# Attention and quantised feed-forward on one core: value matmuls of two key steps in one visit, with a fourth score bank and a ring of three

## The chip, the core and the metric

The kernel runs on one core of a Trainium2 chip. The metric is the device time of one execution in microseconds: 2210.75 us before, the median of three runs from 2209.54 to 2210.94. The engines are TensorE (PE, its weight loads shown as PEld), VectorE (DVE), ScalarE (ACT), GpSimd (POOL) and SyncE (SP), which issues all DMAs.

## The reference

One layer on x of shape (4, 2048, 256), float32. Attention with 16 heads of width 16, causal over the 2048 positions; then a matrix product whose operands are rounded in blocks of 32 to a 6-bit grid.

```python
x = x + attention(layernorm(x), Wq, Wk, Wv, Wo, bo)
x = x + ffn(layernorm(x), weight, bias)

def attention(x, Wq, Wk, Wv, Wo, bo):          # B, C, E = 4, 2048, 256; H, D = 16, 16
    q, k, v = (heads of x @ Wq, x @ Wk, x @ Wv)
    scores = where(causal, q @ k.T, -inf)
    return (softmax(scores / sqrt(E)) @ v) @ Wo + bo

def ffn(x, weight, bias):
    # blocks of 32: scale = max|block| / 7.5, values to the nearest point of the fp6 e2m3 grid
    return dequantised(x) @ dequantised(weight).T + bias
```

## The kernel before, in words

Four heads form a key group; there are 16 groups (4 batches by 4), and each has four query chunks of 512 (a *chunk* k below). For a chunk the kernel walks over the blocks of 128 keys that it can see: 4, 8, 12 or 16 of them, 40 *steps* in a group and 640 in all (`STEPS`, lines 53 to 61). In the first eight or so steps of a chunk, blocks on the diagonal stand between full ones; a diagonal block uses only 512, 384, 256 or 128 columns.

The program runs in *slots*, one for each step and some before and after (line 84). In slot p, each engine does in an order that is written out by hand:

- TensorE (lines 1335 to 1344): for each of the four heads h the score matmul of step p (bf16, transposed scores of 128 keys by up to 512 queries, line 1209), and a share of the slot's units. After h = 1 comes the *value visit*: the values of step p - 2 (line 1226), four fp32 matmuls with 17 output rows each, which lie beside each other in the array, one for each head. Each is issued as two instructions. At the end of the slot come the slot's *items*: projections, transposes, output and feed-forward matmuls.
- A *unit* (line 1191) is a score matmul in the other orientation, 128 queries by up to 512 keys; on the diagonal a mask is added by line 1196. It runs about 21 steps ahead of the step that uses it. VectorE reduces it to one maximum for each query (line 947). The maxima of a chunk are combined, split in three bf16 parts by GpSimd, transposed and loaded as extra rows under the queries, so that the score matmul subtracts them.
- ScalarE (lines 867 to 877) takes exp of each score tile into one of four `probs` buffers (line 805), copies items that it empties, and after a chunk's last step copies the accumulator (line 812).
- GpSimd zeroes the triangle of a diagonal step's probabilities (line 645), one slot after its exponentials, and works on normalisation and on the splitting of projections.
- VectorE (lines 1153 to 1166) takes the slot's units in four shares, with the last slot's items behind the first share, projection work behind the second, and output work behind the third.

PSUM has eight banks. Three hold score tiles in turn: score n waits for exponential n - 3 (line 1208). One holds the accumulator. Four form a *ring* that units and items use in the order of their issue: use n waits until use n - 4 has been emptied by its reader (`emptied`, line 489). A value visit waits for the step's exponentials or, on the diagonal, its mask; the first of a chunk also waits for the copy of the accumulator (line 1224). In ScalarE the first exponential of step s waits for the values of step s - 4 (line 803).

Of the kernel before, what the change touches and what calls it, by code (L numbers as in the profile page):

```python
# [8 lines left out]
ACT = mybir.ActivationFunctionType  # L9
# [7 lines left out]
CHUNK = 512  # L17
# [40 lines left out]
NS = len(STEPS)  # L58
# [3 lines left out]
NPROBS = 4  # L62
# [183 lines left out]
for k in range(NK):  # L246
    p = vector(MAX_DONE[k], 0.3, "maximum", k)
    p = pool(p + 1, 0.9, "split_max", k)
    p = item(p + 1, 0.15, "turn_max", k)
# [3 lines left out]
    p = item(done_at + 1, 0.45, "turn_acc", k)  # L253
# [7 lines left out]
for b in range(B):  # L261
    if b + 1 < B:
        for c in range(QC):
            n = QC * (b + 1) + c
            PROJECTED[n] = place_project(n, 160 * b + 4 + 30 * c)
            assert PROJECTED[n] + 3 < 160 * b + 138 + 6 * c, (n, PROJECTED[n])
    for c in range(QC):
        n = QC * b + c
# [8 lines left out]
for g in range(NG):  # L277
    for c in range(QC):
        p = max(GROUP_STEPS * (g - 1) + 2 + 3 * c, -PRO)
        n = QC * (g // QC) + c  # L280
        p = max(p, PROJECTED[n] + 1)
# [5 lines left out]
SLOTS = range(-PRO, max(p for kind, p in AT) + 3)  # L287


SCORE_BANKS, ACC_BANK, RING_BANKS = [0, 1, 2], 3, [4, 5, 6, 7]  # L290
RING = len(RING_BANKS)

ITEM_KINDS = ("turn_max", "turn_acc", "turn_x", "project", "project_v", "turn_weights", "turn_ctx", "attend", "turn_xd",
              "feed")
# [40 lines left out]
def layer_kernel(nc, x, wq, wk, wv, wo, bo, wf, bf, out):  # L335
# [7 lines left out]
    with ExitStack() as stack:  # L343
# [27 lines left out]
        probs = [sbuf(f"probs{u}", [HG, CHUNK]) for u in range(NPROBS)]  # L371
# [31 lines left out]
        for w in range(2):  # L403
            taken[0] = 0
            s = 1 - w
# [53 lines left out]
        probs_ready = sem("probs_ready")  # L459
# [24 lines left out]
        def wait(eng, semaphore, value):  # L484

            if value > 0:
                eng.wait_ge(semaphore, value)
# [306 lines left out]
        @block.scalar  # L794
        def _(act):
            act.wait_ge(zeros_ready, 1)

            def probabilities(s, h):
                k, kb = STEPS[s]
                a = max(kb - TILES * QCS[k], 0) * P  # L800
                n = s * HG + h
                if h == 0:
                    wait(act, values_done, s - NPROBS + 1)
                act.wait_ge(scores_ready, n + 1)
                nc.scalar.activation(probs[s % NPROBS][:, h, a:CHUNK], bank[SCORE_BANKS[n % 3]][:, a:CHUNK], ACT.Exp,  # L805
                                     scale=SCALE).then_inc(probs_ready, 1)

            def copy_acc(k):
                act.wait_ge(values_done, FIRSTS[k] + SIZES[k])
                if k:  # L810
                    act.wait_ge(for_vector, ITEM_NO["turn_acc", k - 1])
                nc.scalar.copy(acc_sb[:, :], acc_bank).then_inc(acc_copied, 1)  # L812

            def take_turned_max(k):
                act.wait_ge(for_scalar, ITEM_NO["turn_max", k])
                wait(act, row_loaded[k % 2], 48 * (k // 2))
                nc.scalar.copy(max_rows[k % 2][0:LEVELS * HG * TILES, :],
                               ring_bank(ITEM_USE["turn_max", k])[0:LEVELS * HG * TILES, :].bitcast(BF16)[:, 0:P]
                               ).then_inc(scalar_emptied, 1)

            def take_turned_x(n, e):
                act.wait_ge(for_scalar, ITEM_NO["turn_x", n, e])
                nc.scalar.copy(xnT[n % 2][:, e, :], ring_bank(ITEM_USE["turn_x", n, e])).then_inc(scalar_emptied, 1)  # L823

            def take_projected(n, m):
                r = 4 * n + m
                act.wait_ge(for_scalar, ITEM_NO["project", n, m])
                wait(act, low_ready, r - 1)
                nc.scalar.copy(proj[r % 2], ring_bank(ITEM_USE["project", n, m])).then_inc(scalar_emptied, 1)  # L829

            def take_projected_v(n, j):
                act.wait_ge(for_scalar, ITEM_NO["project_v", n, j])
                wait(act, v_stored[n % 2], 16 * (n // 2))
                nc.scalar.copy(v_out[n % 2][:, :, 2 * j:2 * j + 2, :, 0:D],
                               ring_bank(ITEM_USE["project_v", n, j])
                               .rearrange("p (j g h d) -> p g j h d", j=2, g=H // HG, h=HG)
                               ).then_inc(scalar_emptied, 1)

            def take_turned_ctx(n, e):
                w = out_set(n)  # L840
                before, times = before_in_set(n)
                act.wait_ge(for_scalar, ITEM_NO["turn_ctx", n, e])
                if before is not None:
                    act.wait_ge(for_vector, ITEM_NO["feed", before, 1])
                nc.scalar.copy(outT[w][:, e, :], ring_bank(ITEM_USE["turn_ctx", n, e])).then_inc(scalar_emptied, 1)

            def take_turned_xd(n, e):
                act.wait_ge(for_scalar, ITEM_NO["turn_xd", n, e])
                act.wait_ge(for_vector, ITEM_NO["attend", n, 1])
                nc.scalar.copy(outT[out_set(n)][:, e, :], ring_bank(ITEM_USE["turn_xd", n, e])  # L850
                               ).then_inc(scalar_emptied, 1)

            def take_items(p):
                for k, in at("turn_max", p):
                    take_turned_max(k)
                for n, e in at("turn_x", p):
                    take_turned_x(n, e)
                for n, m in at("project", p):
                    take_projected(n, m)
                for n, j in at("project_v", p):  # L860
                    take_projected_v(n, j)
                for n, e in at("turn_ctx", p):
                    take_turned_ctx(n, e)
                for n, e in at("turn_xd", p):
                    take_turned_xd(n, e)

            for p in SLOTS:
                if p == 0:
                    act.wait_ge(wf_ready, 1)
                for h in range(HG):  # L870
                    if 0 <= p < NS:
                        probabilities(p, h)
                    if h == 0:
                        take_items(p - 1)
                for k in range(NK):
                    if p == FIRSTS[k] + SIZES[k] + 1:
                        copy_acc(k)

        @block.vector
        def _(dve):  # L880
# [100 lines left out]
            def take_items(p):  # L981
                for k, in at("turn_acc", p):
                    normalise(k)
                for nothing in at("turn_weights", p):
                    take_turned_weights()
                for n, a in at("attend", p):
                    dve.wait_ge(x_again[out_set(n)], 16 * (before_in_set(n)[1] + 1))
                    add_to_x(n, a, "attend")
                for n, a in at("feed", p):
                    add_to_x(n, a, "feed")  # L990
# [161 lines left out]

            for p in SLOTS:
                units = UNITS_AT.get(p, [])
                for i in range(4):
                    for n in share(units, i, 4):
                        take_unit(n)
                    if i == 0:
                        take_items(p - 1)

                    if i == (1 if p >= 0 else 3):
                        projection_work(p)
                    if i == 2:
                        output_work(p)
                for k, in at("maximum", p):
                    maximum(k)
                for step, in at("weights", p):
                    if step == 0:
                        split_bias()
                        scale_weights()  # L1170
                    else:
                        round_weights()

        @block.tensor
        def _(pe):
# [24 lines left out]
            def scores(s, h):  # L1200
                k, kb = STEPS[s]
                g, qc = divmod(k, QC)
                u, a, n = g % 2, max(kb - TILES * qc, 0) * P, s * HG + h
                if s == FIRSTS[k] and h == 0:
                    pe.wait_ge(row_loaded[k % 2], 48 * (k // 2 + 1))
                    if k == 0:
                        pe.wait_ge(rows_of_ones, 2)
                wait(pe, probs_ready, n - 2)
                nc.tensor.matmul(bank[SCORE_BANKS[n % 3]][:, a:CHUNK],  # L1209
                                 k_rows[u][0:ROWS + LEVELS, h, kb * P:(kb + 1) * P],  # L1210
                                 q_rows[u][0:ROWS + LEVELS, qc, h, a:CHUNK],
                                 start=True, stop=True).then_inc(scores_ready, 1)
# [122 lines left out]
            for p in SLOTS:  # L1335
                units = UNITS_AT.get(p, [])
                for h in range(HG):
                    if 0 <= p < NS:
                        scores(p, h)
                    for n in share(units, h, HG):  # L1340
                        unit(n)
                    if h == 1 and 0 <= p - 2 < NS:
                        values(p - 2)
                items(p)

# [21 lines left out]
```

## Time and profile before

| | before |
|---|---|
| median of three runs | 2210.75 us |
| the profiled execution | 2213.29 us, span 2211.6 us |
| PE busy | 2067.0 us, 93% |
| DVE busy | 1671.3 us, 76% |
| ACT busy | 1342.8 us, 61% |
| POOL busy | 790.3 us, 36% |
| mean granted TensorE clock | 0.978 |

Busy times of the engines overlap. The span is the time from the first to the last instruction of the profiled execution; the execution's own time is a little longer. Matmuls are pipelined: an instruction's time reaches over the start of the next one, so the pace of PE is read from the distance between starts.

### The profile page before, as it was taken

The page shows a single profiled execution, that of the slowest core. Times are in us where ns is not written, and L with a number is a line of the kernel's source. Part 1 is how long each engine was busy: PE and PEld are TensorE (multiplying, and loading weights), DVE is VectorE, ACT ScalarE, POOL GpSimd, SP SyncE. Part 2 cuts the span into 40 slices and gives each one's busy share as a digit, 9 for nine tenths or more (in the row PEclk, how much of TensorE's full clock was granted, in tenths as well). Part 3 has the DMA queues.
Part 4 walks back from the last instruction along what each step waited for, and adds up shares of the span by engine and source line. Part 5 has one row for each costly group of instructions (what it writes and reads, how often), then busy time and mean ns, then how long its engine had stood idle before and what let it go on. Part 6 is the DMA issues. An engine that isn't in the chain of part 4 may idle for free.

```text
span 2211.6 us, 36629 instructions
## 1 busy us (share of the span) xinstructions
PE 2067.0 (93%) x13061; PEld 861.3 (39%) x13061; DVE 1671.3 (76%) x3026; ACT 1342.8 (61%) x2881; POOL 790.3 (36%) x1077
## 2 busy tenths in 40 slices
PE   2789999999999999999999999999999999999973
PEld 1334343343334343443434344343434333343432
DVE  5587777868886868787697877777888888888754
ACT  1136666667665657666675766656676666666640
POOL 4313233241333525334433443535232232323232
PEclk8899999999999999999999999999999999999986
DMA  2341130404031141402213141131303030210111
GB/s 92 120 126 51 48 97 28 109 28 107 6 90 32 57 106 38 125 31 59 85 42 83 45 109 47 47 107 39 108 4 104 4 101 7 71 37 6 51 41 41
DMA packets 180753, 139.79 MB, mean 63 GB/s; under 512 B 56406, under 2 KB 180572, under 8 KB 180572
## 3 DMA queue, kind: packets, MB, share of 16 engines
q1 hardware_dynamic: 180572, 137.45, 22.7%
q8 instruction: 104, 1.70, 0.3%
q14 instruction: 77, 0.63, 0.1%
HBM read 85.73 MB, written 50.86 MB: 62 GB/s over the span
## 4 chain that ended last, share of the span: by engine, by line
PE 81%; DVE 9%; issue 2%; ACT 2%; SPq 2%; POOL 2%; DMA 1%; POOLq 0%; ACTq 0%; DVEq 0%
PE psum L1226 22%; PE psum L1209 22%; PE psum L1191 18%; PE psum L1268 7%; PE psum L1261 5%; DVE max_parts L947 4%; PE psum L1196 2%; PE psum L1251 2%; PE psum L1244 1%; SPq L543 1%; DVE out_shop L1114 1%; DMA shop<-in_L_attn_x 1%; ACT probs L805 1%; PE psum L1290 1%; ACT acc_sb L812 1%
## 5 line engine op out<-in xcount | busy, mean ns | idle before, releaser
L947 DVE TENSOR_REDUCE max_parts<-psum 128x1 f32<-128x512 f32 (+3 forms) x2240 | 1380.1, 667 | 403.4 <-PE psum L1196 210.2
L805 ACT ACTIVATE probs<-psum 128x512 f32<-128x512 f32 (+3 forms) x2560 | 1231.1, 538 | 694.9 <-PE psum L1209 687.4
L1191 PE MATMUL psum<-k_rows,q_rows 96*128 96x512 bf16 (+3 forms) x2560 | 839.3, 349 | 23.8 <-DVE max_parts L947 16.6
L1209 PE MATMUL psum<-q_rows,k_rows 99*128 99x512 bf16 (+3 forms) x2560 | 854.3, 351 | 2.6 <-ACT probs L805 1.9
L1226 PE MATMUL psum<-probs,v_in 128*17 128x512 f32 (+3 forms) x5120 | 594.3, 536 | 10.4 <-ACT acc_sb L812 8.3
L1209 PEld LDWEIGHTS psum<-q_rows,k_rows 99*128 99x128 bf16 x2560 | 237.1, 97 | 621.2 <-ACT probs L805 463.6
L645 POOL TENSOR_SCALAR_AFFINE_SELECT probs<-probs 128x512 f32<-128x512 f32 x256 | 165.0, 645 | 854.2 <-ACT probs L805 854.1
L1191 PEld LDWEIGHTS psum<-k_rows,q_rows 96*128 96x128 bf16 x2560 | 250.6, 98 | 223.5 <-DVE max_parts L947 80.7
L1196 PE MATMUL psum<-maskb,identb 128*128 128x128 bf16 x1024 | 198.7, 220 | 0.0
L1226 PEld LDWEIGHTS psum<-probs,v_in 128*17 128x17 f32 x5120 | 86.1, 95 | 216.7 <-issue 145.8
L1196 PEld LDWEIGHTS psum<-maskb,identb 128*128 128x128 bf16 x1024 | 101.1, 99 | 68.8 <-issue 0.7
L684 POOL CAST neg_max<-neg_rest 128x16 bf16<-128x16 f32 x64 | 12.7, 198 | 223.1 <-DVE neg_rest L954 223.1
L1251 PE MATMUL psum<-ident,shop 128*128 128x128 f32 x160 | 24.8, 305 | 59.4 <-DVE shop L1007 30.3
L676 POOL TENSOR_TENSOR shop<-shop 128x512 bf16<-128x512 f32 x64 | 74.7, 1167 | 5.2
L1261 PE MATMUL psum<-shop,w_q 128*128 128x512 f32 x128 | 64.7, 635 | 2.1 <-ACT shop L823 1.7
L1261 PE MATMUL psum<-shop,w_k 128*128 128x512 f32 x128 | 63.7, 621 | 0.3 <-DVE max_parts L947 0.3
L732 POOL TENSOR_TENSOR out_shop<-out_shop 128x512 f32<-128x512 f32 x28 | 36.8, 1314 | 72.2 <-DVE out_shop L1093 72.1
L829 ACT COPY shop<-psum 128x512 f32<-128x512 f32 x64 | 37.2, 581 | 41.0 <-PE psum L1261 39.4
L675 POOL CAST shop<-shop 128x512 bf16<-128x512 f32 x64 | 40.0, 625 | 61.9 <-DVE shop L1016 60.4
L1268 PE MATMUL psum<-w_v,shop 128*128 128x256 f32 x256 | 61.9, 385 | 0.0
L977 DVE TENSOR_TENSOR out_shop<-psum,out_shop 128x512 f32<-128x512 f32 x56 | 38.2, 683 | 30.9 <-PE psum L1268 30.9
L660 POOL TENSOR_SCALAR shop<-shop,moments,inv_dev 128x256 f32<-128x256 f32 x48 | 58.9, 1236 | 0.6
(116 smaller groups left out, 1353.8 us busy)
## 6 DMA issues: line engine op xcount, KB each, us to landing
qk_scratch<-shop SPq DMA_DIRECT2D x64, 384.0 KB, 2.9
q_rows<-qk_scratch SPq DMA_DIRECT2D x384, 64.0 KB, 2.4
k_rows<-qk_scratch SPq DMA_DIRECT2D x384, 64.0 KB, 2.4
shop<-in_L_attn_x SPq DMA_DIRECT2D x18, 512.0 KB, 4.4
v_scratch<-shop SPq DMA_DIRECT2D x16, 544.0 KB, 3.8
v_in<-v_scratch SPq DMA_DIRECT2D x64, 136.0 KB, 2.4
ctx_scratch<-ctx_out SPq DMA_DIRECT2D x64, 128.0 KB, 1.7
out_shop<-ctx_scratch SPq DMA_DIRECT2D x56, 128.0 KB, 3.1
```

The costliest lines, as they stand in the source:

```text
L645: nc.gpsimd.affine_select(out=tri, in_=tri, compare_op=ALU.is_ge, fill=0.0, base=0, pattern=[[0, HG], [1, P]], channel_multiplier=-1).then ...
L660: ins = nc.gpsimd.tensor_scalar(x_in[n % 2][:, j, :], x_in[n % 2][:, j, :], moments[:, j, 0:1], inv_dev[:, j:j + 1], ALU.subtract, ALU.mult)
L676: nc.gpsimd.tensor_tensor(out=parts[v][:, 2, :], in0=proj[v], in1=parts[v][:, 1, :], op=ALU.subtract).then_inc(low_ready, 1)
L805: nc.scalar.activation(probs[s % NPROBS][:, h, a:CHUNK], bank[SCORE_BANKS[n % 3]][:, a:CHUNK], ACT.Exp, scale=SCALE).then_inc(probs_ready, 1)
L947: nc.vector.tensor_reduce(max_parts[k % 2][:, first:first + heads, t % TILES, c], ring_bank(UNIT_USE[n])[:, 0:heads * width] .rearrange("p ...
L1191: ins = nc.tensor.matmul(dst[:, i * width:(i + 1) * width], q_rows[u][0:ROWS, qc, first + i, t % TILES * P:(t % TILES + 1) * P], k_rows[u] ...
L1196: ins = nc.tensor.matmul(dst[:, (i + 1) * width - P:(i + 1) * width], identb[:, :], maskb[:, :], start=False, stop=True)
L1209: nc.tensor.matmul(bank[SCORE_BANKS[n % 3]][:, a:CHUNK], k_rows[u][0:ROWS + LEVELS, h, kb * P:(kb + 1) * P], q_rows[u][0:ROWS + LEVELS, qc ...
L1226: ins = nc.tensor.matmul(psum[32 * h:32 * h + VW, ACC_BANK, a:CHUNK], v_in[u][:, kb, h * VW:(h + 1) * VW], probs[s % NPROBS][:, h, a:CHUNK ...
L1251: ins = nc.tensor.transpose(ring_bank(use)[:, j * P:(j + 1) * P], t[:, j, e * P:(e + 1) * P], ident[:, :])
L1261: ins = nc.tensor.matmul(ring_bank(use), w[:, e, (m % 2) * P:(m % 2 + 1) * P], xnT[n % 2][:, e, :], start=e == 0, stop=e == EH - 1)
L1268: ins = nc.tensor.matmul(ring_bank(use)[:, j * E:(j + 1) * E], xT[:, e, t * P:(t + 1) * P], w[:, e, :], start=start and e == 0, stop=e == ...
```

## The change

PSUM is dealt out anew: four score banks in place of three, and a ring of three in place of four. The values of an even step and of the odd step after it are issued together, in the visit of the odd slot (step p - 3 and then p - 2); even slots have no visit. ScalarE and VectorE take the last slot's items at the beginning of a slot, before the first exponential and before the first share of units.

```diff
--- before.py
+++ after.py
@@ -287,8 +287,8 @@
 SLOTS = range(-PRO, max(p for kind, p in AT) + 3)
 
 
-SCORE_BANKS, ACC_BANK, RING_BANKS = [0, 1, 2], 3, [4, 5, 6, 7]
-RING = len(RING_BANKS)
+SCORE_BANKS, ACC_BANK, RING_BANKS = [0, 1, 2, 3], 4, [5, 6, 7]
+NSCORE, RING = len(SCORE_BANKS), len(RING_BANKS)
 
 ITEM_KINDS = ("turn_max", "turn_acc", "turn_x", "project", "project_v", "turn_weights", "turn_ctx", "attend", "turn_xd",
               "feed")
@@ -802,7 +802,7 @@
                 if h == 0:
                     wait(act, values_done, s - NPROBS + 1)
                 act.wait_ge(scores_ready, n + 1)
-                nc.scalar.activation(probs[s % NPROBS][:, h, a:CHUNK], bank[SCORE_BANKS[n % 3]][:, a:CHUNK], ACT.Exp,
+                nc.scalar.activation(probs[s % NPROBS][:, h, a:CHUNK], bank[SCORE_BANKS[n % NSCORE]][:, a:CHUNK], ACT.Exp,
                                      scale=SCALE).then_inc(probs_ready, 1)
 
             def copy_acc(k):
@@ -868,10 +868,10 @@
                 if p == 0:
                     act.wait_ge(wf_ready, 1)
                 for h in range(HG):
+                    if h == 0:
+                        take_items(p - 1)
                     if 0 <= p < NS:
                         probabilities(p, h)
-                    if h == 0:
-                        take_items(p - 1)
                 for k in range(NK):
                     if p == FIRSTS[k] + SIZES[k] + 1:
                         copy_acc(k)
@@ -1152,11 +1152,10 @@
 
             for p in SLOTS:
                 units = UNITS_AT.get(p, [])
+                take_items(p - 1)
                 for i in range(4):
                     for n in share(units, i, 4):
                         take_unit(n)
-                    if i == 0:
-                        take_items(p - 1)
 
                     if i == (1 if p >= 0 else 3):
                         projection_work(p)
@@ -1205,8 +1204,8 @@
                     pe.wait_ge(row_loaded[k % 2], 48 * (k // 2 + 1))
                     if k == 0:
                         pe.wait_ge(rows_of_ones, 2)
-                wait(pe, probs_ready, n - 2)
-                nc.tensor.matmul(bank[SCORE_BANKS[n % 3]][:, a:CHUNK],
+                wait(pe, probs_ready, n - NSCORE + 1)
+                nc.tensor.matmul(bank[SCORE_BANKS[n % NSCORE]][:, a:CHUNK],
                                  k_rows[u][0:ROWS + LEVELS, h, kb * P:(kb + 1) * P],
                                  q_rows[u][0:ROWS + LEVELS, qc, h, a:CHUNK],
                                  start=True, stop=True).then_inc(scores_ready, 1)
@@ -1339,7 +1338,8 @@
                         scores(p, h)
                     for n in share(units, h, HG):
                         unit(n)
-                    if h == 1 and 0 <= p - 2 < NS:
+                    if h == 1 and p % 2 and 0 <= p - 3 < NS:
+                        values(p - 3)
                         values(p - 2)
                 items(p)
```

## Rows read from the trace of the kernel before

**Rows 1.** The page: busy time and share by engine, and the granted clock in slices.
```profile
PE 2067.0 (93%) x13061; PEld 861.3 (39%) x13061; DVE 1671.3 (76%) x3026; ACT 1342.8 (61%) x2881; POOL 790.3 (36%) x1077
...
PEclk8899999999999999999999999999999999999986
```

**Rows 2.** Groups by line and shape: busy us, mean ns | idle before.
```profile
L947 DVE TENSOR_REDUCE max_parts<-psum 128x1 f32<-128x512 f32 x1792 | 1130.2, 681 | 223.1 <-PE psum L1191 187.9 <-PE psum L1196 31.7
```

**Rows 3.** Waits: who waited for whom, us in total, times, longest.
```profile
PEld psum L1191 <- DVE max_parts L947: 80.7, 170, 3.2
...
PEld psum L1226 <- POOL probs L645: 10.0, 25, 1.6
...
PE psum L1226 <- ACT acc_sb L812: 8.3, 27, 0.7
```

**Rows 4.** Timeline of one full step: start us, us, engine, line, operation, count.
```profile
1002.82 1.05 PE L1226 MATMUL psum<-probs,v_in 128*17 128x512 f32 x8
...
1003.26 0.61 PE L1226 MATMUL psum<-probs,v_in 128*17 128x512 f32 x4
...
1003.80 0.39 PE L1209 MATMUL psum<-q_rows,k_rows 99*128 99x512 bf16 x1
...
1004.03 0.38 PE L1191 MATMUL psum<-k_rows,q_rows 96*128 96x512 bf16 x1
...
1004.23 2.07 ACT L805 ACTIVATE probs<-psum 128x512 f32<-128x512 f32 x4 [0.80 <-PE psum L1209]
...
1004.25 0.38 PE L1209 MATMUL psum<-q_rows,k_rows 99*128 99x512 bf16 x1
...
1004.45 2.48 DVE L947 TENSOR_REDUCE max_parts<-psum 128x1 f32<-128x512 f32 x4 [0.51 <-PE psum L1191]
...
1005.34 0.38 PE L1191 MATMUL psum<-k_rows,q_rows 96*128 96x512 bf16 x1
...
1005.65 0.13 PEld L1226 LDWEIGHTS psum<-probs,v_in 128*17 128x17 f32 x8 [0.43 <-ACT probs L805]
...
1005.65 1.05 PE L1226 MATMUL psum<-probs,v_in 128*17 128x512 f32 x8
```

**Rows 5.** Timeline of a value visit of 256 columns.
```profile
1117.27 0.63 PE L1226 MATMUL psum<-probs,v_in 128*17 128x256 f32 x8
...
1117.83 0.23 PE L1209 MATMUL psum<-q_rows,k_rows 99*128 99x128 bf16 x1
```

**Rows 6.** Stretches of two steps: start:end, length, busy time by engine, clock, DMA, GB/s.
```profile
135.52:141.50 5.98, 5.78 (x42) 2.08 (x41) 5.98 (x11) 2.82 (x8) 1.27 (x2) 1.00 0.39 108
...
1095.32:1101.23 5.91, 5.91 (x40) 2.07 (x38) 4.42 (x12) 4.34 (x10) 3.15 (x4) 1.00 0.02 2
1101.23:1106.75 5.52, 5.50 (x39) 1.87 (x39) 4.24 (x9) 4.38 (x10) 4.32 (x8) 1.00 0.01 3
1106.75:1112.33 5.58, 5.58 (x40) 2.35 (x40) 4.64 (x9) 3.82 (x10) 0.64 (x1) 1.00 0.09 27
1112.33:1117.27 4.94, 4.94 (x37) 1.94 (x36) 4.91 (x11) 3.44 (x9) 2.56 (x3) 1.00 0.00 0
1117.27:1122.43 5.16, 5.16 (x38) 1.88 (x37) 5.16 (x9) 3.50 (x9) 0.77 (x2) 1.00 0.02 3
1122.43:1127.29 4.86, 4.86 (x33) 1.50 (x32) 4.79 (x10) 3.80 (x9) 0.83 (x4) 1.00 0.00 0
1127.29:1132.98 5.69, 5.69 (x39) 1.94 (x39) 5.18 (x9) 4.67 (x10) 3.31 (x3) 1.00 0.02 2
1132.98:1138.45 5.47, 5.47 (x38) 1.87 (x37) 3.95 (x8) 4.03 (x9) 4.21 (x4) 1.00 0.01 1
1138.45:1144.12 5.67, 5.67 (x35) 1.82 (x34) 4.81 (x9) 4.23 (x9) 0.00 (x0) 1.00 0.01 3
1144.12:1149.71 5.59, 5.32 (x36) 1.81 (x35) 4.50 (x10) 3.98 (x10) 2.35 (x3) 1.00 0.57 137
...
2132.77:2139.21 6.44, 6.44 (x40) 3.13 (x39) 0.36 (x1) 5.16 (x10) 0.00 (x0) 1.00 0.24 83
```

## The prediction

> **What bounds the kernel now.** I read the page first, then the groups of instructions, the waits, one undisturbed step in order of time, and the table of stretches. TensorE is busy for 93% of the span and its granted clock is full through nearly all slices, while VectorE has 76% [rows 1]. The average hides what matters. In steps without projections the table of stretches has PE full, but VectorE is at 4.91 of 4.94 us and 5.16 of 5.16 us in some pairs of steps and at 3.95 of 5.47 us in others [rows 6]. So TensorE sets the pace and VectorE, which reduces the score tiles to maxima ("units") out of the PSUM ring, is level with it for about a third of the pairs. TensorE does wait for VectorE's ring banks, 80.7 us in 170 waits of its weight loads, part of it under running matmuls [rows 3].
>
> **What merging removes.** In the undisturbed step PE starts an instruction of 512 columns every 0.22 us (1004.03 to 1004.25). From the last unit matmul to the first value matmul it is 0.31 us (1005.34 to 1005.65): 0.09 too many. A value visit is two groups of four parallel matmuls 0.44 us apart (1002.82, 1003.26), then the next score matmul at 1003.80: 0.54 after the second group, 0.10 too many [rows 4]. So a visit costs 0.19 us over its streaming, and 640 visits become 320: 320 x 0.19 = 61 us less on PE where PE sets the pace. The second step's groups should follow at 0.44 us.
>
> Whether they do hangs on their weight loads. All eight loads of a visit are done in 0.13 us at its start, and the second group starts 0.44 us after the first, with no gap for a load [rows 4]; a third group isn't shown. Its loads cost nothing (as the second group's) or 0.10 us a pair (the exit bubble again), 0 to 32 us; I take 0, since the second group is the nearest row. The Trainium skill, "TensorE: Matmul & The Clock Gate", section "Step-by-step: what each phase is for", says that a load is pulled ahead of running matmuls if it goes to the background weight buffer or to other row groups; one background buffer would hold the second group, so by this rule the third group's loads could be pulled under the second group's streaming, which gives the same 61 us.
>
> The wait of the first value step of a chunk for ScalarE's copy of the accumulator (8.3 us in 27 waits) [rows 3] goes: PE now gets there a slot later. That is at most 8 us more. The even step's mask on GpSimd also has a slot more, the odd step's none; of those 10.0 us [rows 3] I count nothing, as the odd step ends the visit's wait.
>
> **What it adds: a longer visit over a shorter ring.** VectorE gets nothing new while PE is in a visit. In the chain, PE's last unit before the visit may start once the reduction three uses earlier (four before) has ended; VectorE then has three units in hand. With full widths PE needs 0.31 us from that unit to the visit, 0.98 for the first step's values, 0.88 for the second's, 0.23 for a score, and VectorE starts 0.42 us after the next unit starts (1004.03 to 1004.45): 2.82 us. A reduction takes 0.60 us in a row, (2.48 - 0.68) / 3 [rows 2, 4]; three last 1.80. VectorE therefore starves 1.02 us in each pair. Before, it was 1.94 us of PE against four units or 2.40, so none. With a second step of 256 columns, which costs PE 0.56 us in place of 0.98 [rows 5] and so some 0.44 less, the hole is 0.58. Other VectorE work can lie in the hole (projection statistics of odd slots, normalising, additions to x), which shortens it; units of 384 columns lengthen it. The hole lies between 0 (enough other work there) and 1.02. I take 0.85, nearer to the end with full widths, because in two thirds of the steps the values are full and most of VectorE's other work stands at other places of its slot.
>
> Where PE has that time to spare it costs nothing. Where VectorE is level, the pair lasts VectorE's work plus the hole. So each pair becomes the larger of (its time - 0.19) and (its VectorE time + 0.85). In the ten pairs in a row from 1095.32 [rows 6]: 5.91, 5.52, 5.47 and 5.59 us lose 0.19 each; 5.58 becomes 5.49; 4.94 becomes 5.76; 5.16 becomes 6.01; 4.86 becomes 5.64; 5.69 becomes 6.03; 5.67 becomes 5.66. That is -0.86 and +2.79, or +1.9 us in 54.4. The other half of this key group, with more projection and output matmuls, comes to -0.35. Done for all 319 stretches from 135.52 to 2139.21 (the first and last are in [rows 6]), 113 pairs gain 72 us and the rest lose 35: +37 us, the 61 us already taken off. With a hole of 1.02 it is +65, with 0.4 it is -16, with 0 it is -50.
>
> **The fourth score bank and ScalarE.** Four exponentials take 2.07 us [rows 4], eight 4.14 of a pair of 5.64. While PE is in the long visit ScalarE can have four scores in hand, 2.07 us. From the last score before the visit it is 0.22 us to the last unit, and then the same 2.82 less a few hundredths to the first exponential after it, some 2.8 to 3.0 in all, so ScalarE starves 0.7 to 0.95 and needs 4.9 to 5.1 us a pair: under PE's 5.45. With three banks it would have been 5.4 to 5.6, so the fourth is what keeps the long visit from being ScalarE's bound. It costs the ring its fourth. Cost 0; where two copies of 0.6 us fall in a pair, PE has their matmuls too.
>
> **The moved items.** ScalarE and VectorE now empty the last slot's ring items before the slot's first exponential and unit. PE issues them in that order already, so no engine waits for something later; an exponential is delayed by a copy at most, inside ScalarE's slack (4.0 us busy in pairs of 5.4 [rows 6]). No DMA is issued at another place; SP's waits on scores and values fall at the same slots, as each key group has an even number of steps. ScalarE's wait for the probability buffer four steps back stands behind the next score, which PE issues after that visit anyway. 0.
>
> **Sum.** On the profiled execution, 2213.3 us (span 2211.6): +37 for visits and ring together, -8 at most for the accumulator, of which I take all, gives 2242. The median of the runs is 2.5 below the profiled execution, so 2240.
>
> **Rivals.**
> (a) The hole is filled or hidden, and the bubbles decide: 2160 to 2175, say 2165 (hole 0: 2210.75 - 50, and some of the 8). For it: VectorE has 24% of the span free [rows 1] and some 1 us a pair of work that isn't units (4.64 us busy against seven or eight units). Against it: pairs with VectorE full are those with no spare time for any hole [rows 6], and the order of its work is fixed, so what stands behind a unit can't move ahead into the hole.
> (b) Both effects cancel: a hole of 0.5 to 0.6 gives -5 to +5, and the accumulator's wait makes it 2200 to 2215. For it: many visits have a narrow step [rows 5].
> (c) The three-bank ring costs more than the hole: an item copied by ScalarE takes one of three banks, so VectorE has two units in hand, the hole grows by 0.60, and PE waits also away from visits. If that holds in a third of the pairs, 107 x 0.60 x a half that VectorE decides = 32 us on top: 2270. It decides as soon as a hole exceeds about 1.0. For it: PE already waits 170 times with four banks [rows 3].
> (d) The third group's loads are not hidden: up to 32 us on any of these where PE decides, some 15 on the sum.
> The Trainium skill, "TensorEngine Tiling (Array Packing)", section "PSUM Bottleneck", warns that packing narrow matmuls side by side speeds up TensorE but not the emptying of PSUM, which may then be the bound; this trace agrees in the pairs where VectorE is at 4.91 of 4.94 us [rows 6], and it is the rule that speaks against the change.
>
> **Chances.** The forecast (2220 to 2260) 0.43; (a) 0.26; (b) 0.13; (c) with (d) 0.18. This kernel's measurement tells 0.2%, 4.4 us, from no change. Faster: all of (a) and 0.04 of (b), 0.30; the same 0.08; slower 0.62. The likeliest case has its own range 2220 to 2260; the range for 8 in 10 reaches from (a)'s low end, 2160, to 2285, the sum with a hole of 1.02 and loads that aren't hidden in part.
>
> **What would show it.** Right: value groups come 16 instructions at a time with groups 0.44 us apart and some 1.86 us from first value to next score; pairs such as the one of 5.47 us shrink by 0.19; VectorE has an idle stretch of 0.6 to 1.0 us in each visit, and pairs that were 4.94 and 5.16 us last 5.6 to 6.0; waits of unit matmuls on reductions at least double from 80.7 us; the accumulator's wait is gone. Wrong: if those pairs stay near 5.0 us, VectorE isn't starved and (a) holds; if the third group starts 0.54 us after the second, (d); if waits of score matmuls on exponentials appear in undisturbed steps, ScalarE is the bound and my pricing of the banks was wrong.

## The result, and the profile after

The changed kernel takes 2346.52 us (median of four runs, 2344.76 to 2349.58) against 2210.85 us: ratio 1.0614, 95% interval 1.0595 to 1.0632. That is 136 us slower, outside the range given. The direction was right and the size wrong by more than a factor of four.

The page of the kernel after: busy time by engine, and the granted clock in slices. It answers to [rows 1].

```profile
PE 2132.3 (91%) x13061; PEld 874.6 (37%) x13061; DVE 1666.2 (71%) x3026; ACT 1328.5 (57%) x2881; POOL 789.1 (34%) x1077
...
PEclk8889999999999999999999999999999999999996
```

VectorE does the same work (1666 us) in a longer span. The clock slices look almost the same, but the mean granted clock fell from 0.978 to 0.966.

The waits of the kernel after for VectorE's maxima (us in total, times, longest); the first answers to 80.7 us in 170 waits in [rows 3].

```profile
PEld psum L1190 <- DVE max_parts L947: 381.7, 893, 2.7
...
PE psum L1190 <- DVE max_parts L947: 50.5, 120, 2.2
...
PEld psum L1225 <- POOL probs L645: 8.0, 36, 0.4
```

The masks' row is 8.0 us where it was 10.0. The row of the accumulator's copy, 8.3 us before, has no counterpart any more.

One merged visit and the pair of steps after it, in order of time (start us, us, engine), to be set beside [rows 4]:

```profile
1195.40 1.90 PE L1225 MATMUL psum<-probs,v_in 128*17 128x512 f32 x15
...
1196.27 0.12 PEld L1225 LDWEIGHTS psum<-probs,v_in 128*17 128x17 f32 x4 [0.31 <-issue]
...
1197.24 0.61 PE L1208 MATMUL psum<-q_rows,k_rows 99*128 99x512 bf16 x2
...
1197.67 4.03 ACT L805 ACTIVATE probs<-psum 128x512 f32<-128x512 f32 x8 [1.50 <-PE psum L1208]
...
1198.22 3.68 DVE L947 TENSOR_REDUCE max_parts<-psum 128x2 f32<-128x512 f32 x6 [1.58 <-PE psum L1195]
...
1199.56 0.10 PEld L1190 LDWEIGHTS psum<-k_rows,q_rows 96*128 96x128 bf16 x1 [0.35 <-DVE max_parts L947]
...
1200.16 0.10 PEld L1190 LDWEIGHTS psum<-k_rows,q_rows 96*128 96x128 bf16 x1 [0.49 <-DVE max_parts L947]
...
1200.76 0.10 PEld L1190 LDWEIGHTS psum<-k_rows,q_rows 96*128 96x128 bf16 x1 [0.48 <-DVE max_parts L947]
...
1201.08 0.62 PE L1225 MATMUL psum<-probs,v_in 128*17 128x512 f32 x4
```

The visit lasts 1.84 us from its first value matmul to the next score (1195.40 to 1197.24; 1.86 was predicted). VectorE has then been idle for 1.58 us and ScalarE for 1.50. After that VectorE makes six reductions in a row, and the weight loads of the units stand 0.35, 0.49 and 0.48 us waiting for them. Most of that wait passes under the running score matmul: the unit matmuls themselves start 0.02, 0.15 and 0.15 us late. Here VectorE has only 4.1 us of work in 5.7, and still TensorE waits for it.

The ten pairs of steps of [rows 6], in the kernel after (from one visit to the next; a visit now stands one slot later, so a row shares the values and half of the scores and units with its counterpart):

```profile
1156.12:1161.58 5.46, 5.29 (x35) 1.64 (x33) 4.06 (x8) 3.74 (x9) 4.48 (x8) 1.00 0.01 1
1161.58:1167.96 6.38, 6.21 (x46) 2.68 (x45) 4.90 (x9) 4.62 (x11) 3.36 (x4) 1.00 0.02 5
1167.96:1173.66 5.70, 5.59 (x39) 1.84 (x37) 4.47 (x10) 3.75 (x10) 0.63 (x1) 1.00 0.07 24
1173.66:1179.19 5.53, 5.36 (x39) 1.71 (x37) 4.81 (x10) 3.07 (x9) 2.69 (x3) 1.00 0.00 0
1179.19:1184.99 5.80, 5.62 (x37) 1.75 (x35) 5.00 (x10) 4.25 (x9) 0.83 (x4) 1.00 0.02 3
1184.99:1189.87 4.88, 4.84 (x39) 1.89 (x38) 4.81 (x9) 3.50 (x9) 0.13 (x1) 1.00 0.01 2
1189.87:1195.39 5.52, 5.52 (x35) 1.81 (x34) 4.61 (x9) 4.34 (x10) 5.36 (x5) 1.00 0.01 1
1195.39:1201.08 5.69, 5.69 (x36) 1.80 (x34) 4.11 (x8) 4.19 (x10) 2.04 (x2) 1.00 0.00 1
1201.08:1206.63 5.55, 5.55 (x37) 2.00 (x37) 4.48 (x9) 3.89 (x10) 0.16 (x1) 1.00 0.20 47
1206.63:1213.18 6.55, 5.97 (x39) 2.11 (x38) 5.36 (x11) 3.57 (x11) 4.17 (x5) 1.00 0.36 83
```

Their sum is 57.1 us against 54.4: +2.7, where +1.9 was predicted. Two of the pairs in which VectorE was level went from 4.94 and 5.16 to 5.53 and 5.80 (5.76 and 6.01 were predicted). The sum of this half of a key group came out, but not its rows: the rule had 4.86 and 5.69 become 5.64 and 6.03 where 4.88 and 5.52 were measured, and 5.52 and 5.59 become 5.33 and 5.40 where it was 6.38 and 6.55. Too much for the level pairs and too little for others cancelled here, which is luck. The other half, with most of the projection and output items and 9 of the 12 steps narrower than 512 columns, was priced wrong in sum as well. Five of its pairs before:

```profile
1035.02:1042.64 7.62, 7.62 (x51) 3.84 (x50) 3.80 (x8) 4.92 (x13) 0.64 (x1) 1.00 0.07 20
1042.64:1051.22 8.58, 8.58 (x46) 4.00 (x45) 6.20 (x11) 3.49 (x10) 0.64 (x1) 1.00 0.72 181
1051.22:1059.44 8.22, 8.22 (x49) 4.10 (x48) 4.04 (x7) 4.31 (x10) 4.12 (x5) 1.00 0.70 197
1059.44:1066.96 7.52, 7.52 (x46) 3.34 (x45) 5.11 (x9) 5.64 (x13) 4.13 (x5) 1.00 0.01 4
1066.96:1074.54 7.58, 7.58 (x46) 3.14 (x45) 5.13 (x11) 4.79 (x12) 4.12 (x5) 1.00 0.20 68
```

and the five pairs in their place after (length is the second number, then busy time of PE, PEld, DVE):

```profile
1093.15:1102.98 9.83, 9.42 (x57) 5.20 (x56) 4.93 (x9) 3.97 (x9) 0.63 (x1) 1.00 0.45 110
1102.98:1111.78 8.80, 8.44 (x43) 3.27 (x42) 4.90 (x8) 3.73 (x11) 2.75 (x4) 1.00 0.74 196
1111.78:1120.59 8.81, 8.65 (x48) 4.13 (x46) 4.20 (x7) 5.32 (x11) 3.28 (x5) 1.00 0.13 45
1120.59:1127.20 6.61, 6.44 (x47) 3.06 (x47) 5.09 (x10) 5.40 (x13) 3.01 (x5) 1.00 0.19 62
1127.20:1136.44 9.24, 8.94 (x48) 4.05 (x46) 5.00 (x10) 4.14 (x11) 5.91 (x8) 1.00 0.16 57
```

VectorE is busy for 3.8 to 6.2 us of some 8, far from level, and yet 39.5 us became 43.3. Over the whole run, from the first score of step 0 or 20 of each key group to that of the next, the first halves of the groups went from 1074 to 1180 us and the second halves from 934 to 964.

**Where TensorE starts late.** From all starts of TensorE instructions between the first score and the last value matmul I took the distance between two starts, less what the first streams (its columns at 2.4 GHz and 3 ns; twice the columns for fp32), and summed it by what starts late. A change between value matmuls and others is booked as a bubble of 0.092 us; distances that touch a stretch of low clock stand by themselves.

```
us late before            bubbles   unit  item  score  value  in low clock
before                      118      44    26     30     14       9
after                        59     163    87     26      1      46
items' place only           118      41    25     30     15       7
three-bank ring, single     118      68    49     24     13       8
pair visit, ring of four     59      66    43     74      1      23
before, short maxima        118      13    17     33     17       8
after, short maxima          59      28    19     26      0      11
one ring, single            118      14    17     56     14       7
one ring, pair visit         59      29    39     94      0      20
items' own bank, single     118      60    75     30     11      14
items' own bank, pair        59     151    73     60      1      30
```

The change took 59 us of bubbles and 13 of waits for values away, and brought 119 us of late units, 61 of late items and 37 in low clock: +141, of a span that grew by 136. In pairs of slots with an item the sum of all but bubbles rose from 97 to 237 us, in those without from 32 to 91. The bubble is a count times a price: 1280 changes became 640, at 0.092 us each.

### The profile page after: what moved, and what is told of

The parts are those of the page before. It is cut to its first block, busy times and chain, and to the rows that moved or that the text cites. A ratio compares the mean times of both kernels' runs of the same rounds, so it can differ in the third digit from the quotient of the medians.

```text
span 2347.9 us, 36630 instructions
## 1 busy us (share of the span) xinstructions
PE 2132.3 (91%) x13061; PEld 874.6 (37%) x13061; DVE 1666.2 (71%) x3026; ACT 1328.5 (57%) x2881; POOL 789.1 (34%) x1077
## 4 chain that ended last, share of the span: by engine, by line
PE 68%; DVE 26%; issue 2%; POOL 2%; ACT 1%; DMA 1%; SPq 1%; POOLq 0%; DVEq 0%; ACTq 0%
PE psum L1225 21%; DVE max_parts L947 20%; PE psum L1208 15%; PE psum L1190 13%; PE psum L1267 7%; PE psum L1260 5%; PE psum L1195 2%; PE psum L1250 2%; PE psum L1243 1%; PE psum L1289 1%; DVE out_shop L1114 1%; POOL k_rows L761 1%; DVE stats L995 1%; DMA shop<-in_L_attn_x 1%; DVE out_shop L977 0%
## 5 line engine op out<-in xcount | busy, mean ns | idle before, releaser
L805 ACT ACTIVATE probs<-psum 128x512 f32<-128x512 f32 (+3 forms) x2560 | 1196.1, 543 | 713.7 <-PE psum L1208 708.8
L1190 PE MATMUL psum<-k_rows,q_rows 96*128 96x512 bf16 (+3 forms) x2560 | 861.2, 354 | 77.4 <-DVE max_parts L947 50.5
L1225 PE MATMUL psum<-probs,v_in 128*17 128x512 f32 (+3 forms) x5120 | 547.9, 547 | 0.1
L1190 PEld LDWEIGHTS psum<-k_rows,q_rows 96*128 96x128 bf16 x2560 | 249.4, 97 | 507.7 <-DVE max_parts L947 381.7
L1208 PEld LDWEIGHTS psum<-q_rows,k_rows 99*128 99x128 bf16 x2560 | 242.1, 98 | 401.4 <-issue 169.9
L1225 PEld LDWEIGHTS psum<-probs,v_in 128*17 128x17 f32 x5120 | 118.3, 98 | 234.5 <-issue 147.0
L1243 PE MATMUL psum<-ident,acc_sb 128*128 128x128 f32 x256 | 43.1, 294 | 19.4 <-DVE max_parts L947 17.6
```

The lines of the kernel that those rows point to most:

```text
L1190: ins = nc.tensor.matmul(dst[:, i * width:(i + 1) * width], q_rows[u][0:ROWS, qc, first + i, t % TILES * P:(t % TILES + 1) * P], k_rows[u] ...
L1208: nc.tensor.matmul(bank[SCORE_BANKS[n % NSCORE]][:, a:CHUNK], k_rows[u][0:ROWS + LEVELS, h, kb * P:(kb + 1) * P], q_rows[u][0:ROWS + LEVEL ...
L1225: ins = nc.tensor.matmul(psum[32 * h:32 * h + VW, ACC_BANK, a:CHUNK], v_in[u][:, kb, h * VW:(h + 1) * VW], probs[s % NPROBS][:, h, a:CHUNK ...
L1243: ins = nc.tensor.transpose(ring_bank(use)[:, j * P:(j + 1) * P], acc_sb[:, j * P:(j + 1) * P], ident[:, :])
```

## The experiments

Times are medians, each with its ratio to the kernel before on the same chip. "New order" is the place of the items in the changed kernel.

**The banks alone.** The changed kernel with

```diff
-                    if h == 1 and p % 2 and 0 <= p - 3 < NS:
-                        values(p - 3)
+                    if h == 1 and 0 <= p - 2 < NS:
                         values(p - 2)
```

> The changed kernel with one value visit in every slot again; four score banks, a ring of three and the new place of the items stay. Theory R (the ring): whenever TensorE does something long that yields no unit, a value visit or an item, VectorE lives on the units in hand, and a ring of three leaves it 0.60 us less; the items' holes are there without the long visit. R expects about 2290 us (2250 to 2320). Rival V (the long visit is the cost, with any ring): about the time before, 2205 to 2220. Rival O (items taken at the beginning of the slot delay ScalarE and VectorE): slower than 2230 here and in every kernel that has the new order.

Measured 2257.1 us, 1.0207 (1.0191 to 1.0222): +46, just inside R's range and not V's. It is over O's bound of 2230 too; the run with the order alone settles that. The ring of three costs without any long visit. The waits for maxima, [rows 3] in this kernel:

```profile
PEld psum L1190 <- DVE max_parts L947: 157.8, 421, 2.5
```

**The long visit alone.** The changed kernel with the banks as before:

```diff
-SCORE_BANKS, ACC_BANK, RING_BANKS = [0, 1, 2, 3], 4, [5, 6, 7]
+SCORE_BANKS, ACC_BANK, RING_BANKS = [0, 1, 2], 3, [4, 5, 6, 7]
```

> The changed kernel with the banks as before: three for scores, a ring of four; visits of two steps and the new place of the items stay. R: TensorE keeps the 61 us of the merged visits; the hole in a full visit is 2.82 - 2.40 = 0.42 us in pairs where VectorE is level, and ScalarE with three banks needs 5.4 to 5.6 us a pair: 2185 us (2165 to 2210), faster than before. V: the long visit costs here as well, 2280 or more. O: over 2230.

Measured 2231.0 us, 1.009 (1.0073 to 1.0106). R and V both miss (O's bound is met, and settled by the next run): it is slower than before, by 20 us, and far from 2280. The bubbles went (118 to 59), but against the kernel with only the new order score matmuls start 74 us late in place of 30, units 66 in place of 41, items 43 in place of 25. So TensorE does wait for ScalarE with three score banks, and a ring of four doesn't cover the long visit either:

```profile
PEld psum L1190 <- DVE max_parts L947: 134.3, 311, 2.5
```

**The order alone.** The edit of the two runs above together: single visits, the banks as before, only the place of the items new.

> The kernel before with nothing changed but the place of the items: ScalarE and VectorE take them at the beginning of the slot. R and V: no change, 2206 to 2216 us. O: 2230 or more.

Measured 2204.9 us, 0.9969 (0.9958 to 0.9979), in ten runs: the new order is worth 7 us, where R and V had expected nothing. O is out, and this run is the base of what follows.

**Three and three.** As the banks alone, with `SCORE_BANKS, ACC_BANK, RING_BANKS = [0, 1, 2], 4, [5, 6, 7]` and bank 3 idle.

> As the run with the banks alone (one visit in every slot, ring of three, new place of the items), but with three score banks, one bank left idle. R: the fourth score bank is worth nothing with single visits, so within 8 us of that run, about 2290. V: 2205 to 2220. If ScalarE's scores were what TensorE waits for, this one would be slower than that run by 20 us or more.

Measured 2260.1 us, 1.0219 (1.0204 to 1.0235): the fourth score bank is worth at most 3 us with single visits, which is within the spread; the time itself is 30 us below R's 2290. What the ring lost was given to a side that didn't need it with single visits. What the fourth score bank is worth in time with merged visits no pair of runs isolates.

**Short maxima.** In both kernels,

```diff
-                                        .rearrange("p (h n) -> p h n", h=heads), AX.X, ALU.max).then_inc(unit_used, 1)
+                                        .rearrange("p (h n) -> p h n", h=heads)[:, :, 0:64], AX.X, ALU.max).then_inc(unit_used, 1)
```

> The kernel before, with each maximum taken over the first 64 columns of a head's tile only: this leaves out the rest of the maximum and makes a reduction much shorter than 0.60 us, with the same instructions and waits. Theory R (TensorE's stalls come from VectorE's reductions and a short ring): TensorE's ring stalls of before (starts of units and items some 44 and 25 us late in all) mostly go, so about 2160 us (2145 to 2180). Rival W (the stalls are of another kind: the latency of a wait, ScalarE, data that is late): 2195 or more.

> The changed kernel with the same short maxima (the rest of each maximum is left out). R: with no hole to pay, the 59 to 61 us of merged visits show in full: about 2100 us, 50 to 70 below the short-maximum version of before. Rival V (a long visit costs through something else than VectorE, such as ScalarE or the granted clock): the same as that version or slower.

Measured: before with short maxima 2171.7 us, 0.9819 (0.9804 to 0.9834); after with short maxima 2103.7 us, 0.9517 (0.9502 to 0.9531). Both lie in R's ranges and neither in W's or V's. With VectorE mostly out of the way (its busy time falls to 814 us, below) the same change makes the kernel 68 us faster. The table books 59 less of bubbles, 17 of late values and 7 of late scores, against 15 more of late units, 2 of items and 3 in low clock; the new order, 7 us by itself, is in these. From the changed kernel to this one late units fall from 163 to 28 us, late items from 87 to 19, those in low clock from 46 to 11. This pair of runs shows the cause: in this division of the banks the long visit costs because VectorE's reductions have to be got through the ring, and little else. With three score banks it costs at ScalarE's side too, as the run with the ring of four showed. The page's first line of the changed kernel with short maxima:

```profile
PE 1976.3 (94%) x13061; PEld 915.2 (44%) x13061; DVE 813.9 (39%) x3026; ACT 1304.5 (62%) x2881; POOL 789.2 (38%) x1077
```

and its waits for maxima, where the changed kernel had 381.7:

```profile
PEld psum L1190 <- DVE max_parts L947: 32.1, 56, 6.0
```

**One ring of seven.** Scores, units and items take banks in one order of issue; a use waits for the reader of the use seven before. The core of the edit:

```diff
-SCORE_BANKS, ACC_BANK, RING_BANKS = [0, 1, 2, 3], 4, [5, 6, 7]
+ACC_BANK, RING_BANKS = 7, [0, 1, 2, 3, 4, 5, 6]
...
-    for n in UNITS_AT.get(p, []):
-        UNIT_USE[n] = len(USES)
-        USES.append(("unit", n + 1))
+    for h in range(HG):
+        if 0 <= p < NS:
+            SCORE_USE[p * HG + h] = len(USES)
+            USES.append(("score", p * HG + h + 1))
+        for n in share(UNITS_AT.get(p, []), h, HG):
+            UNIT_USE[n] = len(USES)
+            USES.append(("unit", n + 1))
...
+                elif by == "score":
+                    eng.wait_ge(probs_ready, count)
```

With single visits:

> One value visit in every slot and the new place of the items; the seven banks that aren't the accumulator form one ring that score tiles, units and items use in the order of their issue. With equal counts that is 3.5 banks each, but a slot with one or two units leaves more to the scores and a slot with items more to the ring. R: against the order-only run of 2205 us, a few us either way, 2190 to 2215. Rival C (scores now wait for slow reductions and units for exponentials, each held by the other): 2230 or more.

Measured 2188.9 us, 0.9895 (0.988 to 0.991): faster than both kernels, 16 us below the order-only run and 1 us below R's range. Units start 14 us late in place of 41, items 17 in place of 25, scores 56 in place of 30. That is about half of the gain: between the first score and the last value the profiled execution takes 2000.2 us against 2009.3 in the order-only run. Before the first score, where no score tile needs a bank, it takes 119.4 against 130.0.

With visits of two steps:

> The changed kernel (visits of two steps) with the one ring of seven for scores, units and items. The run with a ring of four and three score banks had paid for the long visit with score stalls (73 us against 30) and the changed kernel with unit stalls (163 against 41). R: sharing seven banks evens this out and is near the better of the two, 2200 to 2235 us; faster than the order-only run (2205) only if the shared ring gives both sides a bank when they need it. Rival C: coupling costs more than it gives, 2260 or more.

Measured 2198.0 us, 0.9948 (0.993 to 0.9965). It is 2 us below R's range. The same seven banks that cost the changed kernel 136 us give a gain of 13 by the medians when they are shared, the new order's 7 included; C is out. But merging still loses 9 us to the single visits: 59 us of bubbles bought with 38 of late scores, 22 of items, 15 of units and 13 in low clock, with 14 of value waits back.

**Work moved into the hole.** `if i == 2:` before `output_work(p)` in VectorE's loop becomes `if i == (1 if p % 2 else 2):`, in the changed kernel and in the one ring with merged visits.

> The changed kernel, with VectorE's output work of odd slots moved one unit forward, to where VectorE starves during the visit of two steps. Theory R (a hole of VectorE in each visit, which other work can fill): about half of the output work of some 5 to 6 us a chunk times 16 chunks lies in odd slots, 40 to 50 us, of which a part was paid as time: 2315 to 2335 us. If the hole isn't what costs, or the work in odd slots already lay in it: 2340 to 2350.

Measured 2343.2 us, 1.0599 (1.0579 to 1.0619), 3 us below the changed kernel: R's range is missed, and the time lies in the other one, 2340 to 2350 (the hole isn't what costs, or this work already lay in it). The run can't tell these two apart. The second halves of the groups gained 10 us by the trace, the first halves lost 3.

> The one ring of seven with visits of two steps (2198 us), with the same output work moved into the visit. R: its unit stalls are only 29 us, its score stalls 94, so little is left for VectorE to gain: 2190 to 2200; under 2189 (the one ring with single visits) only if the scores' waits are themselves VectorE's lateness handed on through the ring.

Measured 2201.4 us, 0.9951 (0.9931 to 0.997): nothing gained. Moving the output work by one unit doesn't fill what is paid for. The starts in low clock are some 40 us late here (20 without the move), with units no later than 30.

**A bank for the items.** Score banks 0 to 2, bank 3 for items, which wait only for the item before, accumulator 4, units in 5 to 7. The core of the edit:

```diff
-            return bank[RING_BANKS[use % RING]]
+            return bank[ITEM_BANK] if use >= ITEM_BASE else bank[RING_BANKS[use % RING]]
```

> The run with a ring of three and three score banks (one visit in every slot, 2260 us), with its idle eighth bank given to the items: units use the ring of three, an item waits only for the item before it. Theory I (most of the ring's cost arises where an item has to wait for a reduction and takes a unit's bank, in the slots with projection and output work): 2215 to 2230 us, near the order-only run of 2205. Rival U (three banks are too few for units alone, in every visit): 2245 or more. Two items in a row now wait for a copy of 0.6 us, which costs up to 20 us in either case.

> The same division of banks (three for scores, three for units, one for items) with visits of two steps and the new place of the items. I: the items' share of the changed kernel's 2346 us goes, but the long visit still meets a ring of three and three score banks: 2260 to 2300. U: the units' waits in the long visit are what costs: 2320 or more. Against the run with a ring of four for both (2231 us), slower in either case.

Measured 2304.8 us, 1.0426 (1.0407 to 1.0444), and 2367.6 us, 1.0699 (1.0681 to 1.0717). Both are above I's ranges and U's lower bounds hold, but the 20 us allowed for items in a row were too few. With the single visit, items start 75 us late against 48 in the three-and-three run, and the stretch from first score to last value is 23 us longer (2081.6 against 2058.7). With the merged visit that stretch is 7 us shorter than in the changed kernel (2144.5 against 2151.7), though scores have one bank fewer and start 60 us late in place of 26. The rest lies outside it: before the first score and after the last value, where items follow each other, the two kernels take 22 and 27 us longer than their partners (in the merged pair 145.0 and 78.1 us against 129.1 and 67.0). So the total time is no test of I. The column of units is a better one: they start 60 us late with the single visit (65 in the three-and-three run) and 151 with the merged one (163 in the changed kernel, which has the fourth score bank). Taking the items out of the ring gave the units little, so by this column I falls and U stands: three banks are too few for the units alone.

## Why the prediction was wrong, point by point

**The bubbles: right.** The table books 59 us less (118 to 59) against 61, and where VectorE is out of the way the whole change gains 68. The third and fourth groups of value matmuls start 0.43 us after the ones before, and the fourth's loads stand at 1196.27, as the third starts. So the loads are hidden, rival (d) is out, and the rule of the Trainium skill on loads that are pulled ahead ("TensorE: Matmul & The Clock Gate", "Step-by-step: what each phase is for") agrees with these rows.

**The accumulator's copy and the masks: about right.** 8 us were taken for the copy, whose wait is gone; all late value matmuls together fell by 13 us. The masks, counted at nothing, still have their waits (8.0 us against 10.0).

**The moved items: priced at nothing, worth 7 us.** The order-only run shows it.

**The score banks: right in sign.** With merged visits scores start 74 us late with three of them and a ring of four, 60 with three and a ring of three, 26 with four. ScalarE is idle for longer than the 0.7 to 0.95 us forecast (1.50 in the visit shown), and still scores are no later than before. With single visits the fourth is worth at most 3.

**The hole: the step that failed.** The hole itself is there and larger than the 0.85 us taken: 1.58 us of idle VectorE in the visit shown above, and 1.14 on average from the first value matmul to 0.45 us after the start of the next unit, over 309 visits of the trace. Some of that is because VectorE had caught up before the visit. The size alone doesn't explain the miss: with 1.14 in place of 0.85 the rule gives +86 in place of +37, so 2291 us, and the profiled execution took 2349.6. What failed is the sentence "Where PE has that time to spare it costs nothing", and with it the rule that each pair becomes the larger of its time less 0.19 and VectorE's time plus 0.85. It sets a whole pair of VectorE's work against a whole pair of TensorE's, as if a surplus of one moment could be worked off in another of the same pair. A ring of three can't carry it. TensorE makes a unit in 0.44 us beside a full score and in less beside a narrow one, VectorE takes 0.60, and after each hole VectorE starts from nothing while TensorE fills three banks and then walks at VectorE's pace until the next visit or item, where VectorE runs dry again. That is the stretch of 5.69 us shown above: by the rule VectorE needed 4.11 + 0.85 = 4.96 us there and TensorE would have decided. The sum of the ten came close (+2.7 against +1.9 us) with errors both ways; the half group predicted at -0.35 us is the one whose like took 106 of the 136 us, 6.6 us in each key group. A second term was put at nothing without a reason: what the ring of three costs where no visit is merged.

**What it cost, from the runs.** From the order-only run, the three-bank ring costs 52 us with single visits (2204.9 to 2257.1) and 115 with merged ones (2231.0 to 2346.5, one score bank more). The merged visit costs 26 us with a ring of four and three score banks and 89 with a ring of three and four score banks, each after its 59 us of bubbles. The two don't simply add: each costs more beside the other. Rival (c), that the ring costs also away from the visits, pointed the right way with 0.18 and priced it at 32 us; its own part, the ring without the long visit, is 52. The reason it gave, that an item takes one of the three banks, carries little of the units' lateness by the runs with the items' own bank.

**The clock: not in the sum.** The mean granted clock gives 2 x (1 - 0.966) x 2348 = 160 us at the 1.2 GHz level against 2 x (1 - 0.978) x 2212 = 97. The same two steps before and after (length, busy times, clock):

```profile
1021.29:1028.43 7.14, 6.18 (x50) 3.14 (x48) 7.11 (x14) 3.34 (x11) 7.14 (x8) 1.00 0.15 42
```

```profile
1073.94:1083.90 9.96, 8.08 (x49) 3.14 (x48) 7.77 (x14) 3.80 (x12) 6.25 (x8) 0.83 0.29 72
```

and the latter in its first two parts:

```profile
1073.94:1078.20 4.26, 2.98 (x17) 1.22 (x15) 4.26 (x8) 2.60 (x9) 4.00 (x5) 1.00 0.17 41
1078.20:1081.60 3.40, 2.90 (x14) 0.63 (x18) 2.22 (x5) 0.12 (x1) 1.35 (x2) 0.50 0.23 70
```

The scores here have 256 and 128 columns, beside full units. VectorE was level in this pair before (7.11 of 7.14 us), so the rule has it become 7.96; it took 9.96. For 4.26 us TensorE waits for bank after bank, busy for 2.98, while VectorE is busy throughout. Then the granted clock is 0.50 (1.2 GHz) for 3.4 us, a merged visit falls into it, its groups of 512 columns start 0.83 and 0.85 us apart in place of 0.43, and VectorE is then idle for 2.14 us. Starts that touch low clock are 37 us later than before, waits in them included. With short maxima that sum is 11, so here the low clock went with TensorE's waits; the one ring with moved output work has some 40 us of it with few late units and 84 us of late scores, so it isn't the units' ring alone. How much the clock adds by itself was not separated.

**The warning of the Trainium skill** ("TensorEngine Tiling (Array Packing)", "PSUM Bottleneck"), that packing speeds up TensorE but not the emptying of PSUM, pointed the right way; it gives no size. The short-maximum pair of runs agrees: the merged visits gain 68 us there and lose 136 with full reductions.

Still open: how the 115 us of the three-bank ring under merged visits divide between the visit's hole, the narrow score steps and the clock. The trace gives late starts by kind, which is a description and not an intervention.

## What to carry to other kernels

Price a buffer by the longest stretch in which its producer is silent and by the ratio of the two rates around it, instruction by instruction; comparing busy times over a window assumes a buffer as large as the window. Before lengthening an engine's uninterrupted visit, make its consumers' work short for a trial: if the gain appears only then, the consumers and the buffer before them, not the visit itself, are the limit. Where two streams share PSUM, try one ring in order of issue: with single visits it was 16 us faster than the better fixed division (about half of it before the first score) and 68 us faster than the other.

## What was not expected of the hardware

Four groups of four column-packed fp32 value matmuls run with 0.43 us between groups and no gap between one step's operands and the next's. Entering and leaving such a group costs 0.09 and 0.10 us whatever the width (512 to 128 columns). And some 62 us more at the low clock level appeared in a kernel whose PE is still busy for 91% of its span, in the profiled execution once in each key group from 941 us on, the one shown above after a stretch where TensorE waits for banks.
